# A rearranged order of one attention step: weighing between the value product and the scores

## The reference

```python
edge = LN1(x + attn(q=x@n2e_q, k=x@n2e_k, v=x@n2e_v, mask=adj.T))      # 8 heads of 64
node = LN2(x + attn(q=x@e2n_q, k=edge@e2n_k, v=edge@e2n_v, mask=adj))
out  = LN3(node + gelu(node@w1 + b1)@w2 + b2)                          # 512 -> 2048 -> 512
return layernorm(x + out)
# attn: softmax(q@k.T / 8, masked where mask == 0) @ v, for each graph and head
```

## Time and profile before

| | us |
|---|---|
| median of 3 runs | 3084.95 (3084.39 to 3085.16) |
| the profiled execution | 3087.05 |
| its span, first to last instruction | 3085.3 |
| TensorE busy | 2926.4 (95%) |
| VectorE busy | 1629.9 (53%) |
| ScalarE busy | 1521.1 (49%) |
| GpSimd busy | 1582.1 (51%) |

### The profile page before, as it was taken

The page is one execution under the profiler, slowest core; times in us unless marked ns, Lnnn a source line. Parts: engine busy times, 40 slices in busy tenths (PEclk is TensorE's granted clock), DMA queues, the critical chain, the costliest instruction groups (busy, mean ns, idle before and its releaser), DMA issues.

```text
span 3085.3 us, 54441 instructions
## 1 busy us (share of the span) xinstructions
PE 2926.4 (95%) x17920; PEld 2416.5 (78%) x17920; DVE 1629.9 (53%) x5018; ACT 1521.1 (49%) x3882; POOL 1582.1 (51%) x1482
## 2 busy tenths in 40 slices
PE   8999999999899998999988999999999999999996
PEld 7787878777777777777777888888888888888885
DVE  6676767667766676677675223333333233333234
ACT  6666666666677777777775322222222222222221
POOL 3757566666577777777772133333332333333324
PEclk9999999999999999999999999999999999999998
DMA  6444444444556565565655211110111111101101
GB/s 196 110 108 110 114 110 117 107 109 110 128 130 166 138 164 145 152 155 143 163 133 136 76 55 55 55 47 14 54 54 48 54 54 54 49 14 53 55 35 61
DMA packets 488338, 295.64 MB, mean 96 GB/s; under 512 B 279040, under 2 KB 410240, under 8 KB 488192
## 3 DMA queue, kind: packets, MB, share of 16 engines
q1 hardware_dynamic: 488192, 294.01, 36.0%
HBM read 159.73 MB, written 67.11 MB: 74 GB/s over the span
## 4 chain that ended last, share of the span: by engine, by line
PE 48%; POOL 24%; issue 16%; ACT 6%; DVE 4%; DMA 1%; SPq 1%; POOLq 0%; DVEq 0%; ACTq 0%
PE proj L1347 23%; PE score L1361 11%; PE proj L1361 11%; POOL source_lo L663 4%; POOL att_tokens L668 3%; POOL att_v L650 3%; ACT att_probs L528 2%; POOL normed L635 2%; POOL normed L637 2%; POOL att_even_sum L635 2%; POOL att_even_sum L637 2%; POOL att_v L648 2%; PE proj L893 2%; POOL att_query_lo L657 1%; POOL att_rstd L626 1%
## 5 line engine op out<-in xcount | busy, mean ns | idle before, releaser
L1293 DVE TENSOR_TENSOR hidden_lo<-hidden,hidden_hi 128x512 fp32r<-128x512 f32 x256 | 217.0, 848 | 946.0 <-ACT hidden_hi L1130 946.0
L1137 ACT ACTIVATE hidden<-proj,ffn_bias 128x512 f32<-128x512 f32 x256 | 176.5, 689 | 1013.4 <-PE proj L1347 1013.4
L528 ACT ACTIVATE att_probs<-att_probs,att_minus_max 128x128 f32<-128x128 f32 x1024 | 398.6, 391 | 315.1 <-DVE att_minus_max L787 312.6
L663 POOL TENSOR_TENSOR source_lo<-source_raw,source_hi 128x512 fp32r<-128x512 f32 x128 | 204.8, 1621 | 295.7 <-ACT source_hi L551 295.7
L101 POOL TENSOR_TENSOR pool_scratch<-pool_scratch 128x1 f32<-128x1 f32 x144 | 30.3, 210 | 544.3 <-DVE ffn_moments L1237 485.3
L776 DVE SCALAR_TENSOR_TENSOR att_q_lo<-proj,att_bias_q,att_q_hi 128x512 fp32r<-128x512 f32 x128 | 96.1, 751 | 285.0 <-ACT att_q_hi L522 284.9
L787 DVE CUSTOM_DVE_ANT_0 att_probs<-score,att_mask 128x128 f32<-128x128 f32 x1024 | 226.4, 286 | 0.0
L893 PE MATMUL proj<-weight_v_hi,source_hi 128*128 128x512 f32 x512 | 212.6, 415 | 13.3 <-DVE weight_v_lo L746 12.4
L940 PE MATMUL score<-att_k_hi,att_q_hi 128*128 128x256 f32 x512 | 158.3, 309 | 65.9 <-DVE att_q_lo L776 65.8
L893 PE MATMUL proj<-source_hi,weight_k_hi 128*128 128x512 f32 x512 | 208.7, 408 | 5.7 <-DVE weight_k_lo L746 5.7
L796 DVE TENSOR_TENSOR att_p_lo<-att_probs,att_p_hi 128x512 f16<-128x512 f32 x256 | 204.8, 841 | 14.2 <-ACT att_p_hi L535 14.2
(11 more groups left out here) (162 smaller groups left out, 8878.7 us busy)
## 6 DMA issues: line engine op xcount, KB each, us to landing
att_tokens<-in_x SPq DMA_DIRECT2D x128, 256.0 KB, 3.0
source_raw<-in_x_t SPq DMA_DIRECT2D x16, 1024.0 KB, 6.0
edges_t<-turned SPq DMA_DIRECT2D x64, 256.0 KB, 2.5
source_raw<-edges_t SPq DMA_DIRECT2D x16, 1024.0 KB, 6.2
att_query_raw<-in_x_t SPq DMA_DIRECT2D x16, 1024.0 KB, 6.9
nodes_t<-turned SPq DMA_DIRECT2D x64, 256.0 KB, 3.1
source_raw<-nodes_t SPq DMA_DIRECT2D x16, 1024.0 KB, 7.5
normed<-nodes SPq DMA_DIRECT2D x16, 1024.0 KB, 5.6
```

The lines of the kernel that those rows point to most:

```text
L528: nc.scalar.activation(probs[:, j, :], probs[:, j, :], ACT.Exp, bias=minus_max[:, j:j + 1], scale=-1.0, accum_out=row_sum[:, side, j:j + 1 ...
L663: nc.gpsimd.tensor_tensor(source_lo[1 - parity][:, c, :], source_raw[:, c, :], source_hi[1 - parity][:, c, :].bitcast(F32), ALU.subtract). ...
L1137: nc.scalar.activation(hidden[:, c % 2, :], up_bank[c % 2][:], ACT.Gelu, bias=bias_1[:, c:c + 1]).then_inc(activated, 1)
L1293: nc.vector.tensor_tensor(hidden_lo[:, c % 2, :], hidden[:, c % 2, :], hidden_hi[:, c % 2, :].bitcast(F32), ALU.subtract).then_inc(hidden_ ...
```

## The change

The order of five engine programs changes; the instructions themselves and their operands do not. On TensorE `weigh` goes from before `values` to behind it, just ahead of the scores, and the four turns of u=3 go to new places. On ScalarE the two halves of the exponentials follow each other, then the high parts of the probabilities, and only then the high parts of key and query. On VectorE `value_rest` moves from the end of a step to just behind the maxima of the next one, and the low parts of the probabilities go ahead of key and query. On GpSimd `inverse_spread` goes ahead of `value_low`, and the query split ahead of `add_bias`. On SP the second store of a turned block goes ahead of the transposes.

```diff
--- before.py
+++ after.py
@@ -464,9 +464,9 @@
                 load_tokens(sp, g + 1, after, 0)
             if not starts(g):
                 store_turned(sp, g - 1, before, 0)
+                store_turned(sp, g - 1, before, 1)
             turn_probabilities(sp, C * g + 2)
             if not starts(g):
-                store_turned(sp, g - 1, before, 1)
                 store_turned(sp, g - 1, before, 2)
                 if before == 1:
                     store_tokens(sp, g - 1, 1 - parity)
@@ -579,36 +579,31 @@
                     value_high(0, 0, 1)
                 if not first:
                     exponentials(n, (u - 1) % 2, 0)
-                key_high(g, own, u)
-                if u == 2 and not starts(g):
-                    centre(act, g - 1, 1 - parity, 0)
-                if u == 3 and not starts(g):
+                    exponentials(n, (u - 1) % 2, 1)
+                turning = u == C - 1 and not starts(g)
+                if turning:
                     copy_turned(act, g - 1, 0)
-                if not first:
-                    exponentials(n, (u - 1) % 2, 1)
-                if u == 2 and not starts(g):
-                    centre(act, g - 1, 1 - parity, 1)
-                query_high(g, own, u)
-                if u == 3 and not starts(g):
-                    copy_turned(act, g - 1, 1)
                 if not first:
                     probabilities_high(n, 0)
                     probabilities_high(n, 1)
+                key_high(g, own, u)
+                if turning:
+                    copy_turned(act, g - 1, 1)
+                query_high(g, own, u)
                 if u < 2:
                     split_source(g, parity, range(2 * u, 2 * u + 2))
                 if u == 2 and not starts(g):
-                    centre(act, g - 1, 1 - parity, 2)
-                    centre(act, g - 1, 1 - parity, 3)
-                if u == 3 and not starts(g):
+                    for b in range(GB):
+                        centre(act, g - 1, 1 - parity, b)
+                if turning:
                     if own == 1 and after == 1:
                         split_queries(g + 1)
                     copy_turned(act, g - 1, 2)
+                    copy_turned(act, g - 1, 3)
                 if u < 2:
                     value_high(g, parity, u + 2)
                 elif not at(g, last_group - 1):
                     value_high(g + 1, 1 - parity, u - 2)
-                if u == 3 and not starts(g):
-                    copy_turned(act, g - 1, 3)
             if own != after and after == 1:
 
                 weights_high(1, "k")
@@ -684,17 +679,17 @@
             split_source(g, parity, range(2, 4))
             add_bias(g, 2)
 
+            if not starts(g):
+                inverse_spread(pool, g - 1)
             value_low(g, parity, 3)
             if not starts(g):
-                inverse_spread(pool, g - 1)
                 if isinstance(g, int) and g % NG == 1:
 
                     pool.wait_ge(norm_in, 2 * 16 * (g // NG + 1))
                 gain_and_shift(pool, g - 1, 1 - parity)
-            add_bias(g, 3)
-
             if own == 1 and after == 1:
                 split_queries(g + 1)
+            add_bias(g, 3)
             if not at(g, last_group - 1):
                 value_low(g + 1, 1 - parity, 0)
                 if own != after:
@@ -825,25 +820,28 @@
 
                     wait(dve, masked, UNIT * C * g)
                     nc.vector.tensor_scalar(mask[:], adj[:], 0.0, MASKED, ALU.is_le, ALU.mult).then_inc(mask_ready, 1)
+                    if not first:
+                        value_rest(g, parity, 1)
+                elif u < C - 1:
+                    value_rest(g, parity, u + 1)
+                elif not at(g, last_group - 1):
+                    value_rest(g + 1, 1 - parity, 0)
+                if not first:
+                    probabilities_low(n, 0)
+                    probabilities_low(n, 1)
                 key_low(g, own, u)
+                query_low(g, own, u)
                 if u == 2 and own != after:
                     if after == 1:
                         weights_low(1, "v")
                     else:
                         feed_forward.low(dve, 0)
                         feed_forward.low(dve, 1)
-                query_low(g, own, u)
-                if not first:
-                    probabilities_low(n, 0)
-                    probabilities_low(n, 1)
                 if u < 2:
                     if not starts(g):
                         add_weighed(dve, g - 1, 1 - parity, before, u + 2)
-                    value_rest(g, parity, u + 2)
                 else:
                     add_weighed(dve, g, parity, own, u - 2)
-                    if not at(g, last_group - 1):
-                        value_rest(g + 1, 1 - parity, u - 2)
             if own != after and after == 1:
                 weights_low(1, "k")
                 weights_low(1, "q")
@@ -950,25 +948,25 @@
                 return
             for u in range(C):
                 turning = u == C - 1 and not starts(g)
+                if turning:
+                    turn(pe, g - 1, 1 - parity, 0)
                 keys(g, parity, own, u)
                 if turning:
-                    turn(pe, g - 1, 1 - parity, 0)
+                    turn(pe, g - 1, 1 - parity, 1)
                 queries(g, parity, own, u)
+                if turning:
+                    turn(pe, g - 1, 1 - parity, 2)
+                if u < 2:
+                    values(g, parity, own, u + 2)
+                elif not at(g, last_group - 1):
+                    values(g + 1, 1 - parity, after, u - 2)
                 if u >= 2:
                     weigh(pe, g, parity, u - 2)
                 elif not starts(g):
                     weigh(pe, g - 1, 1 - parity, u + 2)
                 if turning:
-                    turn(pe, g - 1, 1 - parity, 1)
-                if u < 2:
-                    values(g, parity, own, u + 2)
-                elif not at(g, last_group - 1):
-                    values(g + 1, 1 - parity, after, u - 2)
-                if turning:
-                    turn(pe, g - 1, 1 - parity, 2)
+                    turn(pe, g - 1, 1 - parity, 3)
                 scores(g, u, 0)
-                if turning:
-                    turn(pe, g - 1, 1 - parity, 3)
                 scores(g, u, 1)
 
         over_passes(pe, body)
```

## The result

The changed kernel takes 3127.24 us (3124.46 to 3131.04, four runs) beside 3085.05 of the kernel before: ratio 1.0137, interval 1.0120 to 1.0155. Forecast was 3026, with 2995 to 3076 as the range. Its profiled execution took 3127.03 us, with a span of 3125.2.

A forecast was written before the change was run, and what follows sets the result against it. TensorE, busy 95%, bounds the kernel; an order can win its waits for `q_lo` and ScalarE's copies. Pass 1 31 us, pass 2 39, less 11 for wraps: 59 saved, 3026 us against 3084.95, range 2995 to 3076.

The forecast's parts named there:

- u=3: Fourth step of a group, 14.9 us: turn 0 waits 1.35 us for block 0's shift, turn 1 1.0 for turn 0's copy.
- the wrap: Every second group VectorE returns to the loop's top, idling 2.23 us; scores wait 1.1 us, 11 us for ten (0 to 18).
- u=1: Second step of a group: 10.94 us without a wait, as scores may start at 8.81 and TensorE gets there at 9.52.
- u=2: Third step of a group: 11.1 us, the residual sum carrying four aggregates (0.75 us) and scores waiting some 0.15 (0 to 0.4).
- Ring from maxima to scores: ScalarE and VectorE, from the masked maxima through exponentials, high parts and `q_lo`: scores can start 7.55 us after the maxima.
- Floor: TensorE's time for a step without a wait: 10.94 us, unchanged by the new order because the work is the same.
- Transposes: Probabilities' transposes start when weighing ends and have 6.1 us to land; one lands 3.2 us after issue: cost 0.
- `v_rest`: Moved one step later, behind the maxima on VectorE; the value's low parts still reach u=2's weighing: cost 0, cover 2 us.
- Change of pass and first groups: Weights' low parts stand behind `q_lo`, next pass's first value product waits: 0, between -8 and +8 us, groups 0, 1, 15, 16, 31.
- The collision rival: GpSimd's value split beside `v_rest` and `p_lo`, pair 2.54 us: 2.3 us lost a group, about 3099 us; chance 0.12.
- the sign that the prediction had named: The forecast is wrong if `p_lo` is 2.5 us long outside u=3.
- The clock rival: Two close TensorE waits in u=3 drop the clock in every group: 1.7 us each, 49 in all, 3075 us; chance 0.07.

The follow-up runs named there:

- the short sum: The changed kernel, with the residual sum reading the weighed values from PSUM, scaled in place there, so one SBUF input instead of two: 3049.50 us, ratio 0.9878.

## Why the prediction was wrong

**The step that failed** is the length of the residual sum: "Its length from `attended` to the following instruction is 423.46 - 421.08 = 2.38 us". It was read where the sum starts when GpSimd's instruction is nearly over (the sum takes 0.76 us in that group, and GpSimd has 0.21 left), and carried to a time at which GpSimd still has up to 1.25 us of one to go. The two rows of the kernel before, VectorE's and GpSimd's:

```profile
421.88 0.76 DVE L727 TENSOR_TENSOR normed<-att_attended,att_tokens 128x512 f32<-128x512 f32 x1
```

```profile
420.57 1.52 POOL L663 TENSOR_TENSOR source_lo<-source_raw,source_hi 128x512 fp32r<-128x512 f32 x1 [7.52 <-ACT source_hi L551]
```

At the new place `attended` to maxima is 481.62 - 478.29 = 3.33 us, so the maxima start 2.09 us into the step, not 1.26. This is worth 77.7 us, as the run with the PSUM input shows.

**The second term** is the wrap, priced at 1.1 us. With the short sum ten wraps cost 3.6 each on average (u=0 and u=1 together, over twice the floor): 25 us too little. The walk had VectorE's gap nearly right (2.23; with the short sum 2.47 to 2.94), but not the mask's maker, `p_lo` beside the value split, and the step behind. The two terms make 103 us; u=2 and u=3 were 0.2 better than walked in 27 groups, 6 us. That leaves 97 of the 99 us between forecast (3028) and measured (3127.03) profiled executions; 2 us are not assigned.

**Ring from maxima to scores:** 7.55 walked; in group 9 after it is 489.50 - 481.62 = 7.88, of which 0.19 is `p_lo`'s 1.47. **Floor:** right, u=0 takes 10.90; in pass 2 the floor is 11.0, and u=0 takes 11.8 to 12.0 away from wraps, with the short sum 11.0 to 11.4. **u=1:** forecast at the floor with 0.7 us to spare; 0.83 more in front and 0.33 more in the ring used it up, hence 0.41 of waiting. **u=2:** 12.84 against 12.85, but by the wrong parts: the scores wait 0.71, which turn 0 would have waited for the shift anyway. Block 0 is shifted 503.40 - 491.03 = 12.37 us after the start of u=2, forecast 12.45. **u=3:** turn 1 waited 2.04, not 1.0, for maxima that were late by a sum of 1.75, and then, in 12 of 27 groups, the clock fell.

**Transposes** land as fast as before, at 3.2 and 3.1 us (medians over the stretch of the earlier trace rows), and hold `p_lo` up by 2.4 us in the whole span, TensorE by nothing. **`v_rest`:** one weighing waits for a value, 1.3 us in the last group; otherwise none, as said. **Stores:** no copy waits for one any more, as said. **Change of pass and first groups:** 6 us lost, within the -8 to +8.

**Rivals.** The collision rival (0.12) had the lock and the sign, but not the instruction that decided: in u=1 and u=2 `p_lo` takes some 1.5, not 2.54. It did grow elsewhere: to 2.0 in u=0 of pass 1, to 2.3 to 2.5 in u=0 of pass 2 away from wraps (the sign that the prediction had named), and to 3.2 instead of 2.6 in u=3. What that costs by itself no run shows. It said that a collision decides from 2.2 us a group; the sum's is 77.7 / 27 = 2.9. The Trainium skill, "SBUF — State Buffer", section "Who interferes with whom", says that a VectorE instruction with two SBUF inputs contends with a GpSimd one that reads SBUF, for a port pair that is an exclusive lock, and that a VectorE instruction with at most one SBUF input, outside the two-port modes, does not contend. Both agree with these runs (0.55 us behind GpSimd's end with two SBUF inputs, 0.69 flat with one). The prediction used that rule for one instruction and did not ask it of the other that moved. The clock rival came true in 12 of 27 groups, some 12 x 1.55 = 19 us, behind turn 1's wait; why not in the 12 others with the same wait stays open. Why late weighing was not a rival of its own: the walk priced the slack it takes at nothing, because by it the scores were still in time with 0.7 us left. The kernel before shows 43 us for that alone, and the rearranged order 55 to 78.

## What to carry to other kernels

When an instruction moves, take its length at the new time, not at the old one: look up what GpSimd will be running just then, and list every moved VectorE instruction with two SBUF inputs. A move that leaves 0.7 us of slack in a ring of engines has spent that slack for everything that happens now and then (loop wraps, a norm once a group), so price these against what is left. Where an operand is already in PSUM, reading it there took the collision away at no cost that these runs show.

## What the runs showed of the hardware

The end of the sum follows GpSimd to a hundredth of a microsecond. In the changed kernel 101 of 128 sums started with more than 0.14 us of a GpSimd instruction still to run; each ended 0.54 to 0.56 us after that instruction, whichever of five kinds it was, and the 27 others took 0.69. In the kernel before, 109 of 128 started so as well, but late in GpSimd's instruction (0.16 to 0.24 us left), which hid the law behind a mean of 0.74. And a longer loop body does not only thin out the wraps: with four groups a turn TensorE, which had never waited for issue at a wrap, did so at all four, for 6.9 us, and VectorE's gap there was 3.5 to 4.6 us instead of 2.4 to 2.9.
